# Moving the first attention front into the last state-space unit, and splitting the first weight loads into four groups

## The reference

```python
# block 1: two state-space passes, forward and on the flipped sequence
xn = (x - mu) * rsqrt(var + EPS) * norm_g + norm_b
u, z = split(xn @ Win.T)                       # 256 channels each
u = silu(causal_conv(u, 4 taps) + convb)
dtr, Bm, Cm = split(u @ Wx.T)                  # 8, 16, 16
dt = softplus(dtr @ Wdt.T + bdt)
h = exp(dt * A) * h + (dt * u) * B             # 16 states per channel, step by step
y = (h . C + u * D) * silu(z)
return x + y_fwd @ Wout_f.T + flip(y_bwd @ Wout_b.T)

# block 2: attention and a mixture of experts
h = rmsnorm(x, ln1_w); q, k, v = h @ wqkv.T    # 16 heads of 8, 4 of them for k and v
q, k = rope(q), rope(k)
x = x + softmax(causal(q @ k.T / sqrt(8))) @ v @ wo.T
h = rmsnorm(x, ln2_w); top 2 of 8 experts, each silu(h @ w1.T) * (h @ w3.T) @ w2.T
return x + weighted sum of the experts
```

## Time and profile before

| what | value |
|---|---|
| runs, median | 1783.61 us |
| the profiled execution | 1776.86 us, its span 1775.1 us |
| mean granted TensorE clock in it | 0.878 of 2.4 GHz |
| busy: PE / DVE / ACT / POOL | 1353.8 / 1389.0 / 1064.4 / 1108.9 us |
| L874, GpSimd's products hc | 512 times, 1296 ns |
| L745, VectorE's scans | 448 times (the form that reads dbu), 1205 ns |
| L1891, row maxima | 352 times, 636 ns |

### The profile page before, as it was taken

One profiled execution on the slowest core, in us unless ns is written; L12 is line 12 of the kernel. 1 busy time (PEld: TensorE's weight loads), 2 busy tenths in 40 slices (PEclk: granted clock), 3 DMA queues, 4 the chain that ended last, 5 costly groups with the idle time before them and its releaser, 6 DMA issues. The chain is left out here.

```text
span 1775.1 us, 30877 instructions
## 1 busy us (share of the span) xinstructions
PE 1353.8 (76%) x8880; PEld 982.3 (55%) x8880; DVE 1389.0 (78%) x2234; ACT 1064.4 (60%) x1888; POOL 1108.9 (62%) x1244
## 2 busy tenths in 40 slices
PE   3877887688778787877786528878988888888761
PEld 1566566566656665656565413434665556656561
DVE  0999999999999999999999417677678787777422
ACT  4777677776776676867866023655565655656320
POOL 1677777777778776877777433336366465665525
PEclk9888989898899898998898656888899998999886
DMA  3122302320222023103211021124555454455662
GB/s 126 62 101 97 118 3 95 119 96 18 102 95 115 4 95 119 69 27 119 95 69 45 14 58 51 49 81 143 159 169 184 156 175 150 150 182 158 217 211 69
DMA packets 114411, 184.90 MB, mean 104 GB/s; under 512 B 10385, under 2 KB 87185, under 8 KB 109969
## 3 DMA queue, kind: packets, MB, share of 16 engines
q1 hardware_dynamic: 110192, 175.15, 28.7%
q0 software_dynamic: 4096, 8.40, 1.6%
HBM read 153.03 MB, written 25.89 MB: 101 GB/s over the span
## 5 line engine op out<-in xcount | busy, mean ns | idle before, releaser
L874 POOL TENSOR_TENSOR hc<-hb,cb 128x512 f32<-128x512 f32 x512 | 653.6, 1296 | 208.3 <-DVE hb L745 177.1
L745 DVE TENSOR_TENSOR_SCAN hb<-da,dbu 128x512 f32<-128x512 f32 x448 | 527.6, 1205 | 20.0 <-PE dbu L373 13.6
L622 ACT ACTIVATE da<-dt,a_neg 128x512 f32<-128x512 f32 x512 | 351.8, 716 | 188.0 <-DVE hb L745 160.3
L410 PE MATMUL yp<-ident,hc 128*128 128x128 f32 x2048 | 327.5, 295 | 3.2 <-POOL hc L874 3.1
L410 PEld LDWEIGHTS yp<-ident,hc 128*128 128x128 f32 x2048 | 278.5, 155 | 82.6 <-issue 54.6
L1764 ACT ACTIVATE pt<-scores,lift 128x512 f32<-128x512 f32 x320 | 216.4, 683 | 170.0 <-PE scores L1515 162.2
L1891 DVE TENSOR_REDUCE mx<-ms 128x1 f32<-128x384 f32 (+3 forms) x352 | 218.7, 636 | 114.8 <-PE ms L1477 108.8
L729 DVE TENSOR_TENSOR dbu<-dtu,bp 128x512 f32<-128x512 f32 x384 | 251.3, 684 | 16.1 <-PE bp L398 7.1
L2229 POOL TENSOR_SCALAR_AFFINE_SELECT pt<-pt 128x256 f32<-128x256 f32 (+1 forms) x320 | 118.2, 372 | 197.2 <-ACT pt L1764 196.2
L321 PE MATMUL wp<-xpad,wu 128*128 128x512 f32 x256 | 132.4, 609 | 11.3 <-DVE res L760 6.5
L1477 PE MATMUL ms<-k,q 72*128 72x384 bf16 (+3 forms) x512 | 138.3, 328 | 0.0
(11 more groups left out here) (231 smaller groups left out, 2442.7 us busy)
## 6 DMA issues: line engine op xcount, KB each, us to landing
cb<-c_scratch SPq DMA_DIRECT2D x16, 3072.0 KB, 11.7
wt<-ffn_w_e SPq DMA_DIRECT2D x120, 384.0 KB, 4.2
cb<-c_scratch SPq DMA_DIRECT2D x16, 1024.0 KB, 4.6
q<-q_scratch SPq DMA_DIRECT2D x96, 96.0 KB
xg<-xs_scratch SPq DMA_DIRECT2D x24, 256.0 KB, 3.5
ys_scratch<-ysb SPq DMA_DIRECT2D x24, 256.0 KB
q_scratch<-qp SPq DMA_DIRECT2D x24, 128.0 KB
k<-k_scratch SPq DMA_DIRECT2D x32, 72.0 KB
```

The lines of the kernel that those rows point to most:

```text
L410: last = nc.tensor.matmul(yp[:, c, h * P:(h + 1) * P], src[:, c * P:(c + 1) * P], ident[:, :], is_transpose=True, start=(s < 0 and h == 0 ...
L622: nc.scalar.activation(da[:, s % NDA, :], dt[:, h, :], ACT.Exp, scale=a_neg[:, d, h, n:n + 1]).then_inc(da_done, 1)
L745: nc.vector.tensor_tensor_scan(hb[:, s % NHB, :], da[:, s % NDA, :], src, 0.0, ALU.mult, ALU.add).then_inc(scan_done, 1)
L874: nc.gpsimd.tensor_tensor(hc[:, s % NHC, :], hb[:, s % NHB, :], cb[:, d, s // 2, :], ALU.mult).then_inc(hc_done, 1)
```

## The change

Two edits go together.

The first is at the start of mamba_phase. The weights are loaded in another order and on four semaphores: conv (ident, ncol, win_u, taps of direction 0), proj (col, win_z, wx, wdt), scan (a_neg, sel), late (taps of direction 1, wout). Each engine waits for the group where it first uses it; ScalarE does the norm first and a_neg and sel after the second norm. Its load of the exp and ln table comes after the first two xd copies in the first front.

The second moves the attention front of sequence 0, but v, from ffn_phase into unit (7, 1). The steps are in the constants FIRST_IN to FIRST_POOL. The new functions use the tiles of the state-space phase: win_u for wq and wk, ncol for lnw, half of wu for trig, xpad for ht, t_ln and t_relu for the rotated q and k, t_abs and rem for their sums, u and the other half of wu for the parts. PSUM is wp. ht goes through DRAM (into the last sequence's place of the x2 scratch) to ffn_phase. In ffn_phase the semaphores of that front are raised by the counts already made; SP issues only ident, mask, wv and ht first, the four other first weights after group 0's parts and the rest weights after group 3's; parts_in loads q before k; and the memset of xg goes behind the casts and the other memsets.

```diff
+FIRST_IN = (8, 9)
+FIRST_RSTD = 10
+FIRST_NORM = (20, 22)
+FIRST_XT = 17
+FIRST_HT = 24
+FIRST_PROJ = (19, 19, 22)
+FIRST_ROPE = (20, 21, 24, 24)
+FIRST_ADD = (22, 27)
+FIRST_ACT = (29, 31, STEPS, STEPS)
+FIRST_POOL = (25, 29, 30, STEPS)
...
+        weights = ((conv_loaded, ident[...], w["ident"]), (conv_loaded, ncol[...], w["ncol"]),
+                   (conv_loaded, win_u[...], w["win_u"]), (conv_loaded, wu[:, 0], w["tap_w"][:, 0]),
+                   (proj_loaded, col[...], w["col"]), (proj_loaded, win_z[...], w["win_z"]),
+                   (proj_loaded, wx[...], w["wx"]), (proj_loaded, wdt[...], w["wdt"]),
+                   (scan_loaded, a_neg[...], w["alog"]), (scan_loaded, sel32, w["sel"]),
+                   (late_loaded, wu[:, 1], w["tap_w"][:, 1]), (late_loaded, wout[...], w["wout"]))
...
+        def sp_first_load(sp):
+            sp.wait_ge(ln_norm, count(ln_norm, NB, 0))
+            sp.wait_ge(x_kept, count(x_kept, NB, 0))
+            sp.wait_ge(x1_stored, count(x1_stored, 0, 16))
+            sp.dma_start(xin[:, :, :], x1[0].rearrange("(c p) m -> p c m", p=P)).then_inc(x_loaded, 16)
...
+        def pe_first(pe, k):
+            if k == 0:
+                pe.wait_ge(ffn_loaded, 16 * 4)
+                pe.wait_ge(first_ht, 1)
+                nc.tensor.matmul(wp[:, 0, :], wq[:, 0, :], ht, start=True, stop=True).then_inc(first_proj, 1)
+            elif k == 1:
+                nc.tensor.matmul(wp[:, 1, :], wq[:, 1, :], ht, start=True, stop=True).then_inc(first_proj, 1)
+            else:
+                pe.wait_ge(first_rope, 1)
+                nc.tensor.matmul(wp[0:2 * NKV * HD, 0, :], wk, ht, start=True, stop=True).then_inc(first_proj, 1)
...
             act.preload_act_table_set("natural_log_exp_and_others")
-            act.wait_ge(weights_loaded, n_weights)
+            act_front(act, 0, 0, 13, first=True)
+            act.wait_ge(conv_loaded, 64)
+            for at in range(14, 23):
+                act_front(act, 0, 0, at, first=True)
+            act.wait_ge(scan_loaded, 32)
             nc.scalar.activation(a_neg[...], a_neg[...], ACT.Exp).then_inc(a_ready, 1)
...
+        def dve_first_rope(dve, k):
+            dve.wait_ge(first_proj, (1, 2, 3, 3)[k])
...
+                nc.vector.tensor_tensor(rot[:, k, :], wp[:, k, :], trig[:, k, :], ALU.mult).then_inc(first_rope, 1)
...
+        def pool_first_add(pool, k):
+            src, dst = ((rot, qf), (rotk, kf))[k]
...
+            nc.gpsimd.tensor_tensor(dst, src[:, 0, :], src[:, 1, :], ALU.add).then_inc(first_add, 1)
...
             at = ring(b, g)
-            sp.dma_start(k9[0:PART_ROWS, at:at + 1].rearrange("r h s -> r (h s)"),
...
             for a in range(3):
                 sp.dma_start(q9[a * 3 * HD:(a + 1) * 3 * HD, at].rearrange("r h s -> r (h s)"),
...
+            if b == 0 and g == 0:
+                sp.wait_ge(consts, 4)
+            sp.dma_start(k9[0:PART_ROWS, at:at + 1].rearrange("r h s -> r (h s)"),
...
-            sp_xa(sp, 0, first=True)
-            for dst, name in first_weights:
-                sp.dma_start(dst[...], w[name]).then_inc(loaded, 16)
-            for dst, name in rest_weights:
-                sp.dma_start(dst[...], w[name]).then_inc(rest_loaded, 16)
+            for s, already in made_before["sync"]:
+                sp.sem_inc(s, already)
+            sp.dma_start(ident[...], w["ident"]).then_inc(casts_loaded, 16)
+            sp.dma_start(mask32[...], w["mask"]).then_inc(casts_loaded, 16)
+            sp.dma_start(wv[...], w["wv"]).then_inc(v_loaded, 16)
+            sp.dma_start(ht[:, :], first_ht).then_inc(v_loaded, 16)
```

More of the change, by code:

```diff
@@ L234, in mamba_phase @@
         block = ctx.enter_context(nc.Block())
-        weights = ((ident, "ident"), (win_u, "win_u"), (win_z, "win_z"), (wu, "tap_w"), (wx, "wx"),
-                   (wdt, "wdt"), (wout, "wout"), (col, "col"), (a_neg, "alog"), (ncol, "ncol"), (sel32, "sel"))
-        n_weights = 16 * len(weights)
+        weights = ((conv_loaded, ident[...], w["ident"]), (conv_loaded, ncol[...], w["ncol"]),
[4 more added lines that the diff above has]
+                   (late_loaded, wu[:, 1], w["tap_w"][:, 1]), (late_loaded, wout[...], w["wout"]))
         def y_count(d, s):
@@ L465, in pe_unit @@
                     pe_out(pe, tail[0], s - 10)
+                if not front:
+                    if s == FIRST_XT:
+                        pe_xt(pe, NB)
+                    for k in range(3):
+                        if s == FIRST_PROJ[k]:
+                            pe_first(pe, k)
                 if front:
@@ L643, in act_front @@
                 act_silu_z(act, b, d, 1)
-                act.preload_act_table_set("natural_log_exp_and_others")
+                if not first:
+                    act.preload_act_table_set("natural_log_exp_and_others")
             if at in (27, 30):
@@ L647, in act_front @@
                 act_xd(act, b, d, 1 if at == 27 else 3)
+                if first and at == 27:
+                    act.preload_act_table_set("natural_log_exp_and_others")
             if at == STEPS - 1:
@@ L680, in _ @@
             nc.scalar.activation(sel[:, :, :], sel32, ACT.Copy).then_inc(sel_cast, 1)
-            for at in range(13, STEPS):
-                act_front(act, 0, 0, at)
+            act.wait_ge(proj_loaded, 64)
+            for at in range(23, STEPS):
+                act_front(act, 0, 0, at, first=True)
             act.wait_ge(a_ready, 2)
@@ L785, in dve_unit @@
                     dve_ln_stats_wait(dve, front[0])
+                if not front and s == FIRST_IN[1]:
+                    dve_ln_stats_wait(dve, NB)
                 if tail and tail[1] == 1 and s == 16:
@@ L801, in dve_unit @@
                     dve_ln(dve, front[0], s - 1)
+                if not front and s in FIRST_IN:
+                    dve_ln(dve, NB, s - FIRST_IN[0])
+                for k in range(4):
+                    if not front and s == FIRST_ROPE[k]:
+                        dve_first_rope(dve, k)
                 if front and s in (29, 30):
@@ L875, in pool_hc, with pool_first_part, pool_first @@
                                     ALU.mult).then_inc(hc_done, 1)
+        def pool_first_add(pool, k):
+            src, dst = ((rot, qf), (rotk, kf))[k]
+            pool.wait_ge(first_rope, 2 * k + 2)
+            pool.wait_ge(xd_done, count(xd_done, NB - 1, 8))
+            pool.wait_ge(soft_done, count(soft_done, NB - 1, 16))
+            nc.gpsimd.tensor_tensor(dst, src[:, 0, :], src[:, 1, :], ALU.add).then_inc(first_add, 1)
+        def pool_first_part(pool, k):
+            src, parts, left = ((qf, qp, rot), (kf, kp, rotk))[k // 2]
+            pool.wait_ge(first_act, k + 1)
+            if k % 2 == 0:
+                pool.wait_ge(first_add, k // 2 + 1)
+                nc.gpsimd.tensor_tensor(left[:, 0, :], src, parts[:, 0, :], ALU.subtract).then_inc(first_pool, 1)
+            else:
+                nc.gpsimd.tensor_tensor(parts[:, 2, :], left[:, 0, :], parts[:, 1, :], ALU.subtract).then_inc(first_pool, 1)
+        def pool_first(pool, s):
+            if s == FIRST_RSTD:
+                pool_ln_rstd(pool, NB)
+            for k in range(2):
+                if s == FIRST_ADD[k]:
+                    pool_first_add(pool, k)
+            for k in range(4):
+                if s == FIRST_POOL[k]:
+                    pool_first_part(pool, k)
         def pool_unit(pool, b, d, front=None, tail=None):
             for s in range(STEPS):
+                if not front:
+                    pool_first(pool, s)
                 if front and front[1] == 0 and s == 3:
@@ L1003, in last_plan @@
     return {}
+MADE_BEFORE = ("xa", "in", "in_rstd", "norm", "h0", "ht", "ht_copy", "rope", "qk_add", "part", "qk_part", "parts_out")
 def due_table():
@@ L2284, in _ @@
             nc.gpsimd.memset(k9[:, :, :], 1.0).then_inc(consts, 1)
-            nc.gpsimd.memset(xg[:, :, :], 0.0).then_inc(consts, 1)
+            pool.wait_ge(casts_loaded, 32)
+            nc.gpsimd.tensor_copy(identb[:, :], ident[:, :]).then_inc(casts, 1)
+            nc.gpsimd.tensor_copy(mask[:, :], mask32[:, 0, :]).then_inc(casts, 1)
             nc.gpsimd.memset(vpad[:, :, :, :, :], 0.0).then_inc(consts, 1)
-            pool.wait_ge(consts, 6)
+            pool.wait_ge(consts, 5)
             for n in range(2):
@@ L2290, in _ @@
                     nc.gpsimd.memset(one_columns(n, p), 1.0).then_inc(consts, 1)
-            pool.wait_ge(loaded, n_first)
-            nc.gpsimd.tensor_copy(identb[:, :], ident[:, :]).then_inc(casts, 1)
-            nc.gpsimd.tensor_copy(mask[:, :], mask32[:, 0, :]).then_inc(casts, 1)
+            nc.gpsimd.memset(xg[:, :, :], 0.0).then_inc(consts, 1)
             for s in slots():
```

153 lines of the change are left out of this document (132 added, 21 removed).

## The result

The changed kernel took 1730.90 us, the median of four runs (1728.74 to 1739.85); the kernel before, run in turns with it, took 1782.76 (1779.15 to 1784.44). The ratio is 0.9721, 95% interval 0.9682 to 0.9760: 50 us faster. Forecast were 38.85 us off and 1744.8, with a range of 1737 to 1752; 1730.9 lies under it.

What follows compares the result with a forecast made beforehand. VectorE was taken to bound the steady state-space part, with little overlap at its two ends. 9.65 + 35.7 - 6.5 = 38.85 us off the median 1783.61 gave 1744.8 us, range 1737 to 1752.

Steps and rivals of the forecast that it cites:

- Part 1, the start: Start of the state-space phase: first norm waits only for its statistics; gain 9.65 us, bounds 7.6 and 10.
- cover of 0.8: At the start: ScalarE's preparatory work done at 18.0 us, 0.8 before u's matmuls end at 18.8.
- Part 2, the last unit: Last state-space unit, which takes the attention front: cost 6.5 us (4.02 + 2.50), bounds 1.8 and 13.7.
- VectorE term of 4.02: Last unit: VectorE has no idle time, so its added statistics, aggregates and rotations count in full, 4.02 us.
- GpSimd term of 2.50: End of last unit: GpSimd's added add and subtracts, 3.54 us less 1.04 slack, put 2.50 us on the tail.
- cover of 1.4 to 1.6 us: Last unit: TensorE delivers B 1.4 to 1.6 us before VectorE wants it, so projections were costed at nothing.
- Part 3, the head: Head of the attention phase: first maxima at 1028.1 instead of 1063.83; gain 35.7 us, bounds 31 and 40.
- TensorE in line: Last unit: projections block TensorE and VectorE waits for B; up to +7.2 us, 1752.0; chance 0.13.
- Parts late: Attention head: part 0 or 1 waits behind other loads on three DMA engines; +4.8 us, 1749.6; chance 0.14.
- TensorE at the upper clock at the end: End of last unit: added work keeps TensorE at 2.4 GHz; -4.7 us, 1740.1; chance 0.13.
- The start gated elsewhere: Start: first group or a_neg and sel land no earlier than all did; no 9.65 gain, 1754.4; chance 0.03.
- Rival 5: Attention phase: shifted clock pattern runs TensorE more at 1.2 GHz, making it slower, 1787.2 us or more; chance 0.02.

Runs made afterwards that it cites:

- d1: The changed kernel with the last unit's first two rotary products on VectorE each issued twice; last unit 65.03 us.
- d3: The changed kernel with GpSimd's first rotary add in the last unit issued twice; last unit 63.58 us.
- s3: The changed kernel run again, unaltered, against the kernel before; ratio 0.9826.
- n2: The changed kernel run a third time, unaltered, against the kernel before; ratio 0.9762.
- f3: The changed kernel run a fourth time, unaltered, against the kernel before; ratio 0.9743.
- d2: The changed kernel with the last unit's three projections on TensorE issued twice, six matmuls for three; last unit 63.57 us.

## Why the prediction was wrong in its number

**Part 1, the start: right, and to the digit by luck.** -9.65 forecast, -9.66 between the profiles, -9.5 over all. xn came at 8.97, inside "8 to 9", but 0.6 later than the sum had it: ln_b took 1.04 us where it had taken 0.20, beside VectorE's fold. TensorE's sixteen convolution matmuls gave 0.59 back, 8.81 us after 9.40; over the profiles that hold all sixteen they take 8.7 to 10.2 and overlap between the two starts, so that is a draw. And u came at 20.26, not 18.8: the table load waited 1.44 more (15.64 + 1.89 = 17.53 to 18.97), so the cover of 0.8 was gone. It cost nothing: the second u, at 22.37 where it had been 31.89, still waited 1.42 for its matmuls, against 2.75 before.

**Part 2, the last unit: right in its two terms, with luck in the one at nothing.** +6.5 forecast, +6.1 measured. The VectorE term of 4.02 is 3.79 (from the first dtu to the last scan's end 58.57, was 54.78), and d1 shows the mechanism. The GpSimd term of 2.50 is 2.36 (5.02 less 2.66), and d3 shows that its earlier adds are free. That TensorE costs nothing held too, but not on the terms it was counted on. The forecast took 2.08 us for each projection, at the lower clock, 6.2 in all. In after the three took 3.55 + 1.07 = 4.6, in s3 and n2 3.0, because the clock rose: the unit's mean is 0.74 to 0.77 in the six profiles without the front and 0.80 to 0.88 in those with it. Whether the cover of 1.4 to 1.6 us is there with all three at the lower clock stays open.

**Part 3, the head: right within 1.** -35.7 forecast, -35.04 measured. Maxima came 11.1 us after the first DMA against 10 to 11. The part taken over from before, 7.63 from the first parts issue, is 8.79. Other loads ride on the same queue, as the lower bound had it; that they are the cause is argued and not tested. The second group's first tile came 8.22 us after the first, as forecast, without a wait for parts.

**The base and the untouched stages: the step that failed.** "The median of the runs, 1783.61, lies 6.75 above the profiled one; nothing in the change touches that difference" carried 6.75 us of before's own scatter over to the changed kernel. There the median lies 2.15 below the profiled execution (1730.90, 1733.05). That is 8.9 of the 13.9 us by which the forecast missed. Another 4.0 are the untouched stages between the two profiles, 1605.3 and 1601.3 us, whose change the sum put at nothing. The touched stages account for the last 1.0 (39.84 against 38.85).

Neither figure is a constant of the kernel. In sixteen profiles whose units and attention run the same code, the untouched stages took 1579.1 to 1606.8 us, before's 1605.3 being the second longest; the three profiles of before itself took 1605.3, 1595.1 and 1583.8. The forecast gave its base a range of 3.5 us to either side. Before lay between 1750 and 1785 over all its runs, and the three runs given were at its upper end. With the sum of 38.85 on the means of the other comparisons one gets 1724.7, 1723.1 and 1722.9; measured were 1728.3, 1719.9 and 1718.4. That does not explain the first comparison, though: there before ran at 1782.3, as the forecast had it, and after 49.7 below. Why this difference came out 11 over the sum of the stages, where the four others lie from 3 under it to 5 over it, stays open; scatter of that size is argued from the others and not shown in it.

**The rivals.** TensorE in line: VectorE has no idle time before yg in after, s3, n2, f3, d1 and d2, so it is refuted as far as these draws and what d2 added reach. Parts late: no wait for them between tiles. TensorE at the upper clock at the end: the clock of the last unit did rise, but VectorE is in line there, so it bought nothing. The output stage was 15.17 in this profile, but 15.6 on average against 16.1, 0.5 of the 4.7 us that it would have given. The start gated elsewhere: no. Rival 5 had the right place, TensorE's clock in the stages that nothing touches, but as a price that the change could ask; it is a draw that both kernels make.

## What to carry to other kernels

Forecast a difference stage by stage, and give the absolute time the spread of the stages that the change leaves alone, found from more than one execution: here the last unit repeats to 0.1 us, the start, the output and the head to 1.0 to 1.8, and the rest moves by 28. An engine that is the bound on average can still be waiting for another in the slower draws, so read the releasers of its idle time in two profiles before calling a stage fixed. When one engine's share is doubled to see whether it is in line, read from the trace how much time it really got: here a higher clock took most of the added time away. For a DMA that repeats data over partitions, put the copies inside and the longest real dimension outside.

## What the hardware showed beyond expectation

The same unit of the same kernel took 57.74 or 59.90 us by TensorE's granted clock (0.91 or 0.87), though VectorE is busy for 56.2 or 56.6 of them. More TensorE work raised the clock and bought no time: 12 more matmuls a unit gave a clock of 0.92 and +7.0 us, and the front in the last unit took its mean clock from 0.74 to 0.80 or more.

GpSimd's ln_b, 8 elements a partition, took 1.04 us beside VectorE's product of 1024 elements with two inputs, where it had taken 0.20 us alone. Over the profiles with the new start it took 0.34 to 1.11 us, and in each of the eleven in which VectorE's product began first it ended 0.05 to 0.07 us after that product (8.93 and 8.88 in after, 8.28 and 8.21 in n2). In d2 it came first, at 8.07, and took 0.20. So it looks held until the product is done, not slowed in proportion.
